# Order of the last two feed-forwards: batches alternate, transposes stand inside the second matmuls

## The reference

```python
def _mha(x, y, ...):                       # called twice: a1 (self), a2 (cross to ctx_512)
    ...
    x_out = x + o @ li1_w + li1_b
    h = jax.nn.gelu(_ln(x_out, ln3_g, ln3_b) @ li2_w + li2_b, approximate=False)
    return x_out + h @ li3_w + li3_b

def _L1_ffn_ref(x, Wr, W1, b1, W2, b2):    # one expert of 8, weighted by its softmax probability
    probs = jax.nn.softmax(xf @ Wr.T, axis=-1)
    h = jax.nn.gelu(xf @ W1[eid] + b1[eid], approximate=False)
    y = (h @ W2[eid] + b2[eid]) * probs[:, eid:eid + 1]

x = x + jnp.tanh(g_xattn[0]) * _L0_xattn_ref(_layernorm(x), ctx_512, ...)
x = x + jnp.tanh(g_ffn[0]) * _L0_ffn_ref(_layernorm(x), ...)
x = x + jnp.tanh(g_xattn[1]) * _L1_xattn_ref(_layernorm(x), ctx_512, ...)   # ln1, a1, ln2, a2
x = x + jnp.tanh(g_ffn[1]) * _L1_ffn_ref(_layernorm(x), ...)
```

## Time and profile before

| | before |
|---|---|
| median of 3 runs | 405.53 us |
| lowest, highest run | 402.64, 405.84 us |
| the profiled execution | 402.49 us |
| its span (first to last instruction) | 400.5 us |
| mean granted TensorE clock, share of full speed | 0.957 |
| busy PE, DVE, ACT, POOL | 330.5, 284.5, 270.1, 122.1 us |
| up of a2f's batch 0 begins | 358.82 us |
| last instruction of VectorE ends | 398.05 us |

### The profile page before, as it was taken

How to read it: one execution, slowest core, us unless ns; L and a number is a source line. 1 busy time by engine, 2 the same in 40 slices (tenths; PEclk the granted TensorE clock), 3 DMA queues, 4 the chain that set the end, 5 groups by cost and what they waited for, 6 DMA issues and landing times.

```text
span 400.5 us, 6858 instructions
## 1 busy us (share of the span) xinstructions
PE 330.5 (83%) x2134; PEld 231.5 (58%) x2134; DVE 284.5 (71%) x676; ACT 270.1 (67%) x953; POOL 122.1 (30%) x227
## 2 busy tenths in 40 slices
PE   4889998546397669898998899898977999977796
PEld 4868886313134445464555556575663778854656
DVE  0678679677559976888979879846475987845515
ACT  3478897477157796989899898815215988855060
POOL 1326664248103332332323333311111444421100
PEclk9999999967599998999999999999996999999999
DMA  6800000000059597104950994000000000000001
GB/s 211 324 10 2 0 2 0 1 2 2 0 113 209 120 208 155 37 2 98 212 111 2 200 211 169 2 2 0 2 0 1 2 2 0 3 0 0 2 0 52
DMA packets 6907, 24.74 MB, mean 62 GB/s; under 512 B 1451, under 2 KB 1528, under 8 KB 6136
## 3 DMA queue, kind: packets, MB, share of 16 engines
q1 hardware_dynamic: 6872, 24.31, 25.2%
HBM read 7.00 MB, written 0.52 MB: 19 GB/s over the span
## 4 chain that ended last, share of the span: by engine, by line
PE 49%; DVE 22%; ACT 14%; issue 8%; DMA 3%; POOL 2%; SPq 1%; DVEq 0%; ACTq 0%
PE ps L444 8%; PE ps L543 7%; PE ps L523 7%; DVE nm L1599 5%; PE ps L596 5%; PE ps L579 5%; ACT pring L1222 4%; PE ps L725 4%; PE ps L689 3%; PE ps L470 3%; ACT arena L1096 3%; PE ps L675 3%; DVE xn L1298 3%; PE ps L491 2%; DVE arena L1389 2%
## 5 line engine op out<-in xcount | busy, mean ns | idle before, releaser
L1222 ACT ACTIVATE pring<-ps,nm 128x512 f32<-128x512 f32 x128 | 87.8, 703 | 15.3 <-DVE nm L1599 14.8
L1599 DVE TENSOR_REDUCE nm<-ps 128x2 f32<-128x1024 f32 x64 | 77.6, 1214 | 22.2 <-PE ps L689 21.6
L1096 ACT ACTIVATE arena<-ps,nmx 128x77 f32<-128x77 f32 x256 | 79.1, 343 | 15.3 <-DVE nmx L1373 15.0
L982 POOL TENSOR_SCALAR_AFFINE_SELECT pring<-pring 128x128 f32<-128x128 f32 x128 | 37.7, 294 | 99.8 <-ACT pring L1222 99.7
L689 PE MATMUL ps<-stack 128*128 128x512 f32 x128 | 56.5, 488 | 11.2 <-ACT pring L1222 7.3
L1096 ACT ACTIVATION_READ_ACCUMULATOR arena<-ps,nmx 128x1 f32 x256 | 57.3, 224 | 0.0
L950 POOL TENSOR_TENSOR arena<-arena,rden 128x616 f32<-128x616 f32 x32 | 39.2, 1224 | 52.2 <-DVE rden L1382 52.2
L444 PE MATMUL ps<-ident,pring 128*128 128x128 f32 x320 | 47.0, 276 | 7.7 <-ACT arena L1205 6.3
L444 PEld LDWEIGHTS ps<-ident,pring 128*128 128x128 f32 x320 | 36.9, 141 | 19.7 <-POOL pring L982 12.1
L543 PE MATMUL ps<-arena 128*128 128x128 f32 x320 | 42.3, 280 | 5.7 <-DVE arena L1389 5.7
L543 PEld LDWEIGHTS ps<-arena 128*128 128x128 f32 x320 | 38.8, 191 | 14.2 <-DVE arena L1389 12.9
(11 more groups left out here) (144 smaller groups left out, 516.3 us busy)
## 6 DMA issues: line engine op xcount, KB each, us to landing
stack<-sides SPq DMA_DIRECT2D x32, 256.0 KB, 5.0
stack<-arena SPq DMA_DIRECT2D x16, 256.0 KB, 5.0
stack<-hid SPq DMA_DIRECT2D x12, 256.0 KB, 5.1
wa_sb<-in_wa SPq DMA_DIRECT2D x1, 1536.0 KB, 13.8
early<-in_w SPq DMA_DIRECT2D x2, 512.0 KB, 8.0
stack<-hid SPq DMA_DIRECT2D x8, 128.0 KB, 2.5
arena<-in_wa SPq DMA_DIRECT2D x1, 1024.0 KB, 5.0
pring<-in_wf SPq DMA_DIRECT2D x1, 768.0 KB, 10.6
```

The lines of the kernel that those rows point to most:

```text
L982: pool.affine_select(out=blk, in_=blk, compare_op=ALU.is_gt, fill=0.0, base=0, pattern=[[1, P]], channel_multiplier=-1).then_inc(masked, 1)
L1096: ins = act.activation(Pc[:, i % PC_SLOTS, h * HS:h * HS + M], bank(where[key])[:, h % 4 * HS:h % 4 * HS + M], ACT.Exp, bias=nmx[:, i % 4, ...
L1222: release(act.activation(pring[:, n % 2, i, :], bank(f"S{i}"), ACT.Exp, bias=nm1[:, n % 8, i:i + 1], accum_out=den1[:, n % 8, i:i + 1]), ( ...
L1599: dve.tensor_reduce(nm1[:, n % 8, 2 * u:2 * u + 2], pair(u), AX.X, ALU.max, negate=True).then_inc(nm1_ready, 1)
```

## The change

Only the code behind the second cross attention moves; that attention itself is untouched. `ffn` is split into `ffn_up` and `logits` (the same instructions). TensorE's order becomes: up of a2f for batch 0, transposes of batch 1, down of batch 0, up of batch 1, half of the down of batch 1, transposes of f1's batch 0, the other half; then f1 in the same manner. ScalarE runs the four Gelus of batch 0 without a copy between them, and a copy of transposes stands in front of each batch's Gelus. VectorE builds the residual batch by batch (`a2_residual`, three steps that each wait for the one before) instead of over both. The preload of Exp and all behind it stay as they are.

```diff
-            ffn("a2f", 0)
+            ffn_up("a2f", 0)
             ln_transposes("a2f", 1)
-            ffn("a2f", 1)
             ffn_down("a2f", 0)
-            ffn_down("a2f", 1)
+            ffn_up("a2f", 1)
+            ffn_down("a2f", 1, range(0, 2))
+            ln_transposes("f1", 0)
+            ffn_down("a2f", 1, range(2, NT))
             pe.wait_ge(loaded["wf1"], 16)
-            ln_transposes("f1", 0)
-            ffn("f1", 0)
+            ffn_up("f1", 0)
+            logits(0)
+            ffn_down("f1", 0, range(0, 2))
             ln_transposes("f1", 1)
-            ffn("f1", 1)
-            ffn_down("f1", 0)
+            ffn_down("f1", 0, range(2, NT))
+            ffn_up("f1", 1)
+            logits(1)
             ffn_down("f1", 1)
...
-            for site, names in (("a2f", ("a2_ln3_g", "a2_ln3_b")), ("f1", None)):
-                if site == "a2f":
-                    preload(ACT.Gelu)
-                else:
-                    ln_evac(site, 0, names)
-                gelu(site, 0, names)
-                gelu(site, 1)
+            preload(ACT.Gelu)
+            gelu("a2f", 0)
+            ln_evac("a2f", 1, ("a2_ln3_g", "a2_ln3_b"))
+            gelu("a2f", 1)
+            for b in range(NB):
+                ln_evac("f1", b)
+                gelu("f1", b)
             preload(ACT.Exp)
...
+            def a2_residual(b, step):
+                if step == 0:
+                    did(dve.tensor_tensor(xb[:, b, :, :], x1[:, b, :, :], row4("a2_li3_b"), ALU.add))
+                elif step == 1:
+                    did(dve.tensor_tensor(xb[:, b, :, :], xb[:, b, :, :], xo[:, b, :, :], ALU.add))
+                else:
+                    did(dve.scalar_tensor_tensor(r[:, b, :, :], xb[:, b, :, :], tg[:, 1:2], r[:, b, :, :],
+                                                 ALU.mult, ALU.add))
+                settle()
...
+            for step in range(3):
+                a2_residual(0, step)
+            a2_out(0)
+            ln_stats("f1", 0, r)
+            for step in range(3):
+                a2_residual(1, step)
+            ln_norm("f1", 0, r)
+            a2_out(1)
+            ln_stats("f1", 1, r)
+            ln_norm("f1", 1, r)
```

More of the change, by code:

```diff
@@ L570, in cross, with ffn_up @@
                         filled(pe.matmul(bank("B")[:, 0:3], ones[:, :], wsum[:, :], start=True, stop=True), "wsum")
-            def ffn(site, b):
+            def ffn_up(site, b, parts=range(NF)):
                 w1, w2, _ = FFN_W[site]
                 pe.wait_ge(xnT_ready, nthT(site, b))
-                for k in range(NF):
+                for k in parts:
                     res = f"S{k}"
@@ L580, in ffn, with logits @@
                            ("up", site, b, k))
[L581 to L586, removed]
+            def logits(b):
+                claim(pe, "T0", ("logits", b), read_by=(logits_ready, b + 1))
+                for t in range(NT):
+                    m = pe.matmul(bank("T0")[:, t * 8:(t + 1) * 8], xnT[:, b, t * P:(t + 1) * P],
+                                  wf1_sb[:, 2 * HID:2 * HID + 8], start=True, stop=True)
+                filled(m, ("logits", b))
             def ffn_down(site, b, tiles=range(NT)):
@@ L812, in down_beside_fold @@
                 return pair_issued
-            ffn("a1f", 0)
+            ffn_up("a1f", 0)
             ln_transposes("a1f", 1)
             fold("a2", 0, down_beside_fold(0))
-            ffn("a1f", 1)
+            ffn_up("a1f", 1)
             fold("a2", 1, down_beside_fold(1))
@@ L1113, in cross, with gelu @@
                         ln_evac("a2f", 0, ("a2_ln3_g", "a2_ln3_b"))
-            def gelu(site, b, names=None):
+            def gelu(site, b):
                 for k in range(NF):
-                    if k == 2 and b == 0:
-                        ln_evac(site, 1, names)
+                    if site == "a1f" and k == 2 and b == 0:
+                        ln_evac("a1f", 1, ("a1_ln3_g", "a1_ln3_b"))
                     key = ("up", site, b, k)
@@ L1238, in _ @@
             preload(ACT.Gelu)
-            gelu("a1f", 0, ("a1_ln3_g", "a1_ln3_b"))
+            gelu("a1f", 0)
             gelu("a1f", 1)
@@ L1645, in _ @@
             cross("a2")
[L1646 to L1654, removed]
             def a2_out(b):
@@ L1660, in a2_out @@
                 settle()
-            ln_both("f1", a2_out, r)
+            add_to_xb(1, "a2")
+            ln_stats("a2f", 1, xo)
+            ln_norm("a2f", 1, xo)
+            for step in range(3):
[8 more added lines that the diff above has]
+            ln_norm("f1", 1, r)
             for b in range(NB):
```

## The result

The changed kernel takes 401.48 us in the median of 20 runs (400.68 to 403.3), the kernel before, timed beside it, 406.12 us (402.25 to 408.94). The ratio is 0.9912 with a 95% interval of 0.9888 to 0.9936, 3.6 us less. The direction holds, and by the ratio "within 1%" holds too, though its interval reaches to 1.1%; the gain is four times what I gave, and the reason for most of it is not in my sum.

What follows compares the result with a forecast made beforehand. The prediction saw TensorE's chain with 4.35 us of waits, then the path behind the last Gelu, as the bound; 0.24 us (earlier Gelu) plus 0.67 us (VectorE's wait) gave 405.53 - 0.9 = 404.6 us, range 401.7 to 406.0.

Steps and rivals of the forecast that it cites:

- the tail's shape: Behind the second cross attention: four TensorE waits (4.35 us) go, TensorE ends 3.87 us earlier, the last Gelu only 0.24 us.
- the path behind the last Gelu: Kernel's end: Exp table load, probabilities and bias put the first output instruction 5.56 us after the last Gelu, at 394.90.
- The rival by which TensorE sets the end: Kernel's end: with the Exp and VectorE path hidden, all 3.87 us come off, giving 401.7 us; chance 0.06.
- the up: Feed-forward matmuls of a2f and f1 on TensorE: each up of one batch was taken at 3.70 us.
- I put the gain on the median: Whole kernel: the 0.9 us gain was taken off the 405.53 us median, though the profiled execution took 402.49 us.
- the clock as a rival for slower only: New tail: TensorE's clock falls as ahead of the cross attention, losing 3.4 us, giving 408.0 us; chance 0.04.
- the range: Whole kernel: 401.7 to 406.0 us, from the rival with TensorE setting the end up to the highest run, 405.84.
- the norm of f1's batch 0: Ahead of f1's first transposes: TensorE could start at about 373.65 and comes at 374.04, so 0.4 us in hand.
- my two cases: GpSimd's power beside VectorE's residual: no cost (taken), or taking turns, 1.01 us on the path and a gain of 0.3 us.
- the new wait: Ahead of a2f's second down: TensorE idles 0.77 us for the last Gelu of batch 1.
- The stores: Kernel's end, issued 1.1 us apart instead of 1.8: no cost taken; if they take turns, 0.9 us lost, 405.5 us, chance 0.08.

Runs made afterwards that it cites:

- e6_f1_only: Changed kernel with a2f put back to both ups, then both downs, so only f1 alternates; 409.45 us, ratio 1.0073 to the kernel before.
- e4_f1_pair: Changed kernel with f1 put back to both ups, then both downs, f1's first transposes still inside a2f's down; 401.05 us, ratio 0.9892 to the kernel before.
- e1_before: The kernel before, unchanged, run and profiled again; 405.39 us, ratio 0.9997 to the kernel before.
- e5_fill_all: Kernel before, order kept, with matmuls nobody reads in all five TensorE waits behind the second cross attention; 403.0 us, ratio 0.9949 to the kernel before.

## Why the prediction was partly right

- **Right: the tail's shape.** The last up starts 21.17 us after a2f's transposes (21.23 in my sum, 21.47 before), the path behind the last Gelu is 5.55 us to the first output instruction (5.56), TensorE is done well ahead of it, and batch 1's output follows without a wait. The rival by which TensorE sets the end would have given a tail of 37.8 us; it is 40.36, and e6_f1_only and e4_f1_pair show the path at work from both sides.
- **Mis-sized, by 0.4 us: the up, above all.** At full clock the tail is 1.33 us shorter, where I had 0.90. I used 3.70 us for every up. That is the figure for an up that TensorE begins from a standstill; behind other matmuls the chain gives it 3.44 to 3.45 us, and 2.04 to 2.05 us instead of 1.79 to the first half of a down. For all but the last up this evens out, but the last up carries the last Gelu 0.25 us forward. The eight output instructions without a gap take 2.16 us instead of 1.13 + 1.12, another 0.09 us.
- **Wrong: "I put the gain on the median".** My own execution lay 3.04 us below the median, and I wrote that nothing in the trace says why and went on. That gap was in good part the effect itself: three of the four other profiles of before have a tail that is 2.96 to 3.26 us longer than the one that I had. Its head, too, is short, 358.82 us against a mean of 360.07. The step took a profile at the fast end for a typical one.
- **Wrong: the clock as a rival for slower only.** I wrote that the old tail "ran at 1.00 throughout" and priced a fall for the new tail at 3.4 us. The weak places were in the old tail: 1.27 and 0.87 us of waiting around 0.63 us of transposes, and 2.13 and 0.68 us around another 0.64 us. The change removes the second and half of the first, and the loss of 3.0 to 3.3 us that three of five profiles show goes with them.
- **Luck: the range.** That 402.0 us, by the ratio, lies within my range owes nothing to the sum. The range reached down to 401.7 for the rival by which TensorE sets the end, which the runs refute; what carried the time there was the clock, which I had let work only the other way.
- **Right, with little room: the norm of f1's batch 0.** It ended at 375.40 and TensorE came to it at 375.96, 0.4 us after it could have, as computed. The power of GpSimd in between was neither of my two cases:

```profile
372.06 0.68 DVE L1449 TENSOR_TENSOR sides<-x,rows_sb 128x512 f32<-128x512 f32 x1
...
372.23 1.38 POOL L946 TENSOR_TENSOR rstd<-var,minus_half 128x4 f32<-128x4 f32 x1 [8.03 <-DVE var L1296]
...
372.77 0.69 DVE L1451 TENSOR_TENSOR sides<-sides 128x512 f32<-128x512 f32 x1
...
373.50 0.75 DVE L1453 SCALAR_TENSOR_TENSOR r<-sides,tg,r 128x512 f32<-128x512 f32 x1
...
374.29 1.11 DVE L1303 TENSOR_SCALAR xn<-r,mv,rstd 128x128 f32<-128x128 f32 x4
```

It took 1.38 us instead of 1.01. The residual's first step, on two operands in SBUF, began 0.17 us ahead of it and ended at 372.74; the power ended 0.87 us after that, and the second step was not held up. The Trainium skill, "SBUF — State Buffer", section "Who interferes with whom", says that of two such instructions the later one stands until the first is done. These rows agree with it in part: the power, which came second to the first step, took longer, but the second step, also with two operands in SBUF, took its usual 0.69 us while the power was still under way. The longer power cost nothing here, since the third step ended after it.
- **Right: the new wait** ahead of a2f's second down, from 373.14 to 373.91, is the 0.77 us of the sum. The stores cost nothing that can be seen: the span ends 2.44 us after the last output instruction, 2.46 before.

## What to carry to other kernels

Where one profile lies at an end of the spread of its runs, the spread is part of the kernel and has to be explained before a gain is added to the median: look for places where TensorE waits twice with little work between, since the clock that is lost behind them can cost as much as the waits themselves (2.97 us behind 2.83 us of waits in e1_before). And when work is moved ahead of a point, ask what stood behind that point as a cover: the down of f1's batch 0, moved before the last up, uncovered a path on two other engines, and leaving it behind (with one tile of it in the wait) was worth 2 us more by the tails of the profiles, 38.29 against 40.36 us.

## What the runs showed of the hardware

In the tails a clock at half speed came behind waits of 1.27 and 0.87 us, and of 2.14 to 2.28 and 0.69 us, each pair with 0.6 to 0.8 us of transposes between, in some executions and not in others of one kernel; the same matmuls then took 5.24 to 6.49 us instead of 3.70. Single waits of 0.6 to 0.8 us were not followed by a fall in any tail here, nor was the single wait of 1.27 us in the changed kernel, nor were the 0.60 and 0.69 us around transposes in the one profile of e4_f1_pair. In the head, near 283 us, the clock did fall behind a single wait of 1.27 us in e1_before and e5_fill_all, so that these waits do not by themselves say where it falls. A power of GpSimd on 128x4 elements took 1.38 us where a VectorE instruction with two inputs in SBUF was under way when it began, 1.01 us in the same place of the kernel before, and 1.01 to 1.14 us elsewhere.
